# Probabilities times values in quarter-width matmuls instead of zero-padded full-width ones

## The chip, the cores and the metric

The kernel runs on one core of one Trainium2 chip, as one program. The metric is the device time of one execution in microseconds (us). The kernel before has two runs, 3971.99 and 3973.98 us, and their median, 3972.98 us, is the time to compare with.

## The reference, cut to what matters

The reference adds four blocks to x one after another: an attention, a linear layer with a low-rank update, a bidirectional state-space mixer and the linear layer again. Only the attention is touched. It has batch 8, 512 tokens, width 1024, 32 query heads of 32 and a single key and value head that all query heads share:

```
b, t, d = x.shape                                  # 8, 512, 1024
q = (x @ wq_w.T + wq_b).reshape(b, t, H, HD)       # H = 32, HD = 32
k1 = (x @ wk_w.T + wk_b).reshape(b, t, 1, HD)[:, :, 0, :]
v1 = (x @ wv_w.T + wv_b).reshape(b, t, 1, HD)[:, :, 0, :]
scores = einsum('bqhd,bkd->bhqk', q, k1) / sqrt(HD)
weights = softmax(where(causal, scores, -inf), axis=-1)
attn = einsum('bhqk,bkd->bqhd', weights, v1)       # the product that is changed
return attn.reshape(b, t, H * HD) @ wo_w.T + wo_b
```

## The kernel before, in words

The program has two parts. `attention_program` comes first and writes x1 to memory; `mixer_program` does all the rest. Each engine has its own instruction list, written out by hand, and semaphores order the engines among each other. No planner is involved.

`attention_program` first splits the weights into high and low parts (setup). Then `row(b, nxt)` handles one batch and prepares the next one: it is called once with b = None, seven times in a loop on the chip, and once for the last batch. All engines meet at a barrier between two rows.

Inside a row, the 32 heads form 8 groups (GROUPS) of 4 heads (GH), which together have 128 output features, one PSUM partition for each. The 512 query tokens form 4 tiles of 128. For query tile i, only the i + 1 key tiles up to the diagonal are computed. A *unit* is as many heads of one query tile as fit in 512 columns of scores: 4 heads for i = 0, 2 heads for i = 1, and 1 head for i = 2 and i = 3. So a group has 1 + 2 + 4 + 4 = 11 units (PER_GROUP), a row has 88, and the eight batches have 704.

The engines work on units in a pipeline. In step s of TensorE's loop (the loop over `range(UNITS + AV_LAG)`), TensorE does in this order:

- the scores of unit s: per head one matmul with q_stack as the weights and k_stack streaming (L524), and one that adds the causal mask (L526);
- in the first three units of a group, a third of the query projection of the next group (`q_part`, L464 to L466 of `split_product`);
- in one unit of a group, `finish_spread` (L484), which turns the softmax denominators of the group before;
- the transposes of the probabilities of unit s - 2 (L544);
- probabilities times values of unit s - 3 (L557), the code that is changed.

Between them, VectorE takes the maximum of each row of scores (L398), ScalarE takes the exponential (L305), and VectorE copies the transposed probabilities out of PSUM to `probs_t` (L408), which L557 waits for. `finish_scale` on VectorE (L355) reads the finished group of outputs, 128 partitions by 512 tokens in PSUM bank 6 or 7, and divides it by the denominators.

In L557 the stationary operand (the weights) is a slice of 128 columns of `v_pad`, and `probs_t` streams through in 128 columns. `v_pad` has 7 * 32 columns for each key tile: the value tile of 32 columns in the middle and zeros on both sides. A window of 128 columns that starts at `lead = (GH - 1 - j) * HEAD` puts the values at the columns of head j and zeros at those of the other three heads. Thus each matmul writes all 128 PSUM partitions of its query tile, and adds zero to those of the other heads; all heads and key tiles of a query tile form one accumulation, which starts at head 0, key tile 0. The operands are float32, and the profile shows two load-and-matmul pairs for each such product in the code. The zeros are written once at the start by GpSimd (L106), the values once per row by VectorE (L451).

Of the kernel before, what the change touches and what calls it, by code (L numbers as in the profile page):

```python
# [5 lines left out]
P = 128  # L6
# [8 lines left out]
def attention_program(nc, x, wq_t, wkv_t, wo_t, bq, bkv, kv_scale, bo, ident, ident_b, causal_b, wq_split, x1):  # L15

    BATCH, T, D = x.shape
    HEAD = wkv_t.shape[1] // 4
    TILES, CH = T // P, D // P
    GROUPS, GH = D // P, P // HEAD  # L20
# [7 lines left out]
    S_RING, P_RING, T_RING, STAT = 3, 3, 2, 8  # L28
# [12 lines left out]
    with ExitStack() as ctx:  # L41
        def sb(name, shape, dt=F32):
            return ctx.enter_context(nc.sbuf_tensor(name, shape, dt))
# [11 lines left out]
        q_hi, q_lo = sb("q_hi", [P, T], F32R), sb("q_lo", [P, T], F32R)  # L55
        q_stack = sb("q_stack", [KROWS, 2, GH, T], F32R)
        k_stack = sb("k_stack", [KROWS, T], F32R)
        v_pad = sb("v_pad", [P, TILES, 7 * HEAD])
        probs = sb("probs", [P, P_RING, T])
        probs_t = sb("probs_t", [P, T_RING, T])  # L60
        neg_max = sb("neg_max", [P, STAT, GH])
# [27 lines left out]
        with nc.Block() as block:  # L89
            @block.sync  # L90
            def _(sp):
                for n, (src, _, _) in enumerate(staged):
                    if n >= 2:
                        sp.wait_ge(staged_lo, n - 1)
                    sp.dma_start(stage(n), src).then_inc(stage_in[n % 2], DMA)
                    if 0 <= n - 3 < CH:

                        for part, w in enumerate(staged[n - 2][1:]):
                            sp.dma_start(wq_split[part, :, :, n - 3, :].rearrange("g p m -> p g m"),
                                         w.bitcast(F32).rearrange("p (g m) -> p g m", g=GROUPS)).then_inc(wq_out, DMA)  # L100
                sp.wait_ge(wq_out, 2 * CH * DMA)

            @block.gpsimd
            def _(pool):
                nc.gpsimd.memset(neg_half[:, :], -0.5).then_inc(setup_done, 1)
                nc.gpsimd.memset(v_pad[:, :, :], 0.0).then_inc(setup_done, 1)  # L106
                pool.wait_ge(params_in, 7 * DMA)
                nc.gpsimd.tensor_tensor(bkv_scaled[:, :], bkv_sb[:, :], kvs_sb[:, :], ALU.mult).then_inc(bkv_ready, 1)
                pool.wait_ge(setup_done, 2)

            @block.scalar
            def _(act):
                params = [(ident_sb[:, :], ident), (identb_sb[:, :], ident_b), (causal_sb[:, :], causal_b),
                          (bo_rows[:, :], bo), (bq_sb[:, :], bq), (bkv_sb[:, :], bkv), (kvs_sb[:, :], kv_scale)]
                for dst, src in params:
                    act.dma_start(dst, src).then_inc(params_in, DMA)
                for n, (_, hi, _) in enumerate(staged):
                    act.wait_ge(stage_in[n % 2], DMA * (n // 2 + 1))
                    nc.scalar.copy(hi, stage(n)).then_inc(staged_hi, 1)
                act.wait_ge(bkv_ready, 1)  # L120
                act.wait_ge(params_in, 7 * DMA)

            @block.vector
            def _(dve):
                for n, (_, hi, lo) in enumerate(staged):
                    dve.wait_ge(staged_hi, n + 1)
                    nc.vector.tensor_tensor(lo, stage(n), hi.bitcast(F32), ALU.subtract).then_inc(staged_lo, 1)
                dve.wait_ge(setup_done, 2)
                dve.wait_ge(params_in, 7 * DMA)

            @block.tensor
            def _(pe):
                pe.wait_ge(params_in, 7 * DMA)
                pe.wait_ge(staged_lo, len(staged))
# [22 lines left out]
        def row(b, nxt):  # L157
# [7 lines left out]
            with nc.Block(no_gpsimd_drain=True) as block:  # L165
# [168 lines left out]
                def _(dve):  # L334
# [58 lines left out]
                    if b is not None:  # L393
                        for s in range(UNITS + T_LAG):
                            if s < UNITS:
                                g, i, heads, n = unit(s)
# [45 lines left out]
                    if nxt is not None:  # L442
                        x_low(3)
                        dve.wait_ge(kv_done, 1)
                        nc.vector.tensor_copy(k_stack[:, :], att[0:KROWS, :]).then_inc(khi_done, 1)
                        dve.wait_ge(khi_done, 1)
                        low = slice(2 * HEAD, 3 * HEAD)
                        nc.vector.tensor_tensor(k_stack[low, :], att[low, :], k_stack[low, :].bitcast(F32),
                                                ALU.subtract).then_inc(k_done, 1)
                        dve.wait_ge(vt_ready, 1)  # L450
                        nc.vector.tensor_copy(v_pad[:, :, (GH - 1) * HEAD:GH * HEAD],  # L451
                                              ps[:, KV, 0:TILES * HEAD].rearrange("p (k d) -> p k d", d=HEAD)).then_inc(v_done, 1)
                        q_low(GROUPS)
                        dve.wait_ge(k_done, 1)
                        dve.wait_ge(v_done, 1)
# [5 lines left out]
                def _(pe):  # L461
# [52 lines left out]
                    if b is not None:  # L514
                        for s in range(UNITS + AV_LAG):
                            if s < UNITS:
                                g, i, heads, n = unit(s)
                                if s % PER_GROUP == 0 and g:
                                    pe.wait_ge(qs_in, g * STACK_DMAS * DMA)
                                if s >= S_RING:  # L520
                                    pe.wait_ge(exp_done, s - S_RING + 1)
                                for m, j in enumerate(heads):
                                    cols = ps[:, s % S_RING, m * n:(m + 1) * n]
                                    nc.tensor.matmul(cols, q_stack[:, g % 2, j, i * P:(i + 1) * P], k_stack[:, 0:n],  # L524
                                                     start=True, stop=False)
                                    mm = nc.tensor.matmul(cols[:, n - P:n], identb_sb[:, :], causal_sb[:, :], start=False, stop=True)  # L526
                                mm.then_inc(s_ready, 1)
                                q_unit = s % PER_GROUP
                                if q_unit < Q_UNITS and g + 1 < GROUPS:
                                    if q_unit == 0 and g:  # L530
                                        pe.wait_ge(qlo_done, g)
                                        if g >= 2:
                                            pe.wait_ge(spread_done, g - 1)
                                    q_part(g + 1, range(q_unit * CH // Q_UNITS, (q_unit + 1) * CH // Q_UNITS))
                                if (done := finishing(s, SPREAD_AT)) is not None:
                                    finish_spread(done)
                            if T_LAG <= s < UNITS + T_LAG:
                                u = s - T_LAG
                                g, i, heads, n = unit(u)
                                pe.wait_ge(exp_done, u + 1)  # L540
                                if u >= T_RING:
                                    pe.wait_ge(pt_done, u - T_RING + 1)
                                for k in range(n * len(heads) // P):
                                    mm = nc.tensor.transpose(ps[:, 4 + u % T_RING, k * P:(k + 1) * P],  # L544
                                                             probs[:, u % P_RING, k * P:(k + 1) * P], ident_sb[:, :])
                                mm.then_inc(pt_ready, 1)
                            if s >= AV_LAG:
                                u = s - AV_LAG
                                g, i, heads, n = unit(u)
                                pe.wait_ge(pt_done, u + 1)  # L550
                                if u % PER_GROUP == 0 and g >= 2:
                                    pe.wait_ge(att_done, g - 1)
                                for m, j in enumerate(heads):
                                    for k in range(i + 1):
                                        lead = (GH - 1 - j) * HEAD
                                        cols = slice(m * n + k * P, m * n + (k + 1) * P)
                                        mm = nc.tensor.matmul(ps[:, 6 + g % 2, i * P:(i + 1) * P], v_pad[:, k, lead:lead + P],  # L557
                                                              probs_t[:, u % T_RING, cols],
                                                              start=(j == 0 and k == 0), stop=(j == GH - 1 and k == i))
                                mm.then_inc(av_done, 1)  # L560
                    if nxt is not None:
                        transposes(0)
# [875 lines left out]
```

## Time and profile before

| What | Value |
|---|---|
| Runs | 3971.99 and 3973.98 us, median 3972.98 us |
| Profiled execution | span 3969.6 us; no other time of it is recorded |
| TensorE matmuls (PE) | busy 3404.7 us, 86% of the span |
| Weight loads (PEld) | busy 2841.5 us, 72% |
| VectorE (DVE), ScalarE (ACT), GpSimd (POOL) | 53%, 28%, 16% |
| L557, probabilities times values | 5120 matmuls and 5120 weight loads |
| Attention | until about 2180 us; the mixer program fills the rest |

The busy time of a matmul includes its passage through the array, so that matmuls which follow each other closely overlap in the records. The step from the start of one to the start of the next tells how fast the engine works; the duration of one record does not. In a merged line of the timeline, "x8" with a length of 1.06 us means eight instructions from the start of the first to the end of the last. A line of the timeline is: start in us, length in us, engine, line, operation, out<-in, weights (rows*columns), the streamed shape, how many, and idle time of the engine before it with what ended it.

### The profile page before, as it was taken

How to read it: one execution, taken by the hardware profiler on the slowest of the kernel's cores; microseconds unless marked ns; L12 is line 12 of the kernel's file. 1: busy time of each engine (PE TensorE's matmuls, PEld its weight loads, DVE VectorE, ACT ScalarE, POOL GpSimd, SP SyncE). 2: the span in 40 equal slices, each digit the busy share in tenths (PEclk: the TensorE clock that was granted, in tenths of full speed). 3: DMA queues.
4: the chain of work that ended last, by engine and by line, in shares of the span. 5: the costliest groups of instructions: out<-in, count | busy, mean ns of one | idle time of the engine just before them, and what ended most of it. 6: DMA issues, size and time to landing. Idle time of an engine off the chain costs nothing. (4 is left out here: it accounts for less than half of the span.)

```text
span 3969.6 us, 53353 instructions
## 1 busy us (share of the span) xinstructions
PE 3404.7 (86%) x20224; PEld 2841.5 (72%) x20224; DVE 2089.3 (53%) x3582; ACT 1116.5 (28%) x2964; POOL 618.2 (16%) x754
## 2 busy tenths in 40 slices
PE   1898998998989989989999778878787878787868
PEld 1786887887868878878788356757575757666656
DVE  3463663654636626546466236555565646464633
ACT  2341442423414414324244013121212121121221
POOL 0001001000010010000100033223232323232311
PEclk9999999999999999999999778888898988888878
DMA  6322222222222222132221400000101010101000
GB/s 213 96 75 94 79 63 96 78 70 89 75 83 75 67 93 84 60 101 79 73 75 46 154 22 22 13 31 11 33 9 34 6 38 6 37 3 41 1 21 22
DMA packets 105455, 234.99 MB, mean 59 GB/s; under 512 B 20170, under 2 KB 38858, under 8 KB 105202
## 3 DMA queue, kind: packets, MB, share of 16 engines
q1 hardware_dynamic: 100544, 228.22, 18.6%
q8 instruction: 180, 2.95, 0.3%
q10 hardware_dynamic: 4658, 3.22, 0.3%
q14 instruction: 73, 0.60, 0.0%
HBM read 139.10 MB, written 41.94 MB: 46 GB/s over the span
## 5 line engine op out<-in xcount | busy, mean ns | idle before, releaser
L305 ACT ACTIVATE probs<-ps_attn,neg_max 128x128 f32<-128x128 f32 (+3 forms) x1024 | 534.8, 526 | 1070.5 <-DVE neg_max L398 1045.5
L557 PE MATMUL ps_attn<-probs_t,v_pad 128*128 128x128 f32 x5120 | 696.3, 277 | 17.5 <-DVE probs_t L408 15.9
L557 PEld LDWEIGHTS ps_attn<-probs_t,v_pad 128*128 128x128 f32 x5120 | 626.7, 192 | 33.6 <-DVE probs_t L408 28.2
L398 DVE TENSOR_REDUCE neg_max<-ps_attn 128x1 f32<-128x384 f32 (+3 forms) x704 | 449.8, 639 | 315.9 <-PE ps_attn L526 313.7
L408 DVE COPY probs_t<-ps_attn 128x512 f32<-128x512 f32 (+1 forms) x704 | 447.1, 636 | 272.4 <-PE ps_attn L544 272.4
L1182 PE MATMUL ps_mixer<-m_w_hi,m_xt_hi 128*128 128x512 f32 x1024 | 429.0, 419 | 77.1 <-DVE m_xt_lo L1021 77.1
L524 PE MATMUL ps_attn<-k_stack,q_stack 96*128 96x128 f32 (+3 forms) x1024 | 371.1, 398 | 72.9 <-issue 50.6
L1183 PE MATMUL ps_mixer<-m_w_hi,m_xt_lo 128*128 128x512 f32 x1024 | 415.6, 406 | 0.0
L1184 PE MATMUL ps_mixer<-m_w_lo,m_xt_hi 128*128 128x512 f32 x1024 | 414.2, 405 | 0.0
L544 PE MATMUL ps_attn<-ident_sb,probs 128*128 128x128 f32 x2560 | 397.5, 274 | 0.0
L544 PEld LDWEIGHTS ps_attn<-ident_sb,probs 128*128 128x128 f32 x2560 | 285.2, 142 | 20.3
L1182 PEld LDWEIGHTS ps_mixer<-m_w_hi,m_xt_hi 128*128 128x128 f32 x1024 | 203.1, 198 | 130.6 <-DVE m_xt_lo L1021 87.7
L524 PEld LDWEIGHTS ps_attn<-k_stack,q_stack 96*128 96x128 f32 x1024 | 203.0, 201 | 78.5 <-issue 69.3
L246 POOL COPY att<-inv_den 128x512 f32<-128x512 f32 x64 | 39.3, 615 | 1395.8 <-DVE inv_den L348 1395.8
L526 PE MATMUL ps_attn<-causal_sb,identb_sb 128*128 128x128 bf16 x1024 | 233.2, 235 | 27.0 <-issue 27.0
L1021 DVE TENSOR_TENSOR m_xt_lo<-ps_mixer,m_xt_hi 128x512 fp32r<-128x512 f32 x192 | 125.7, 687 | 231.0 <-ACT m_xt_hi L933 231.0
L1184 PEld LDWEIGHTS ps_mixer<-m_w_lo,m_xt_hi 128*128 128x128 f32 x1024 | 202.6, 198 | 45.0
L1183 PEld LDWEIGHTS ps_mixer<-m_w_hi,m_xt_lo 128*128 128x128 f32 x1024 | 203.6, 199 | 42.7 <-issue 1.9
L464 PE MATMUL ps_attn<-xn_hi,wq_hi 128*128 128x512 f32 x512 | 221.0, 432 | 0.0
L466 PE MATMUL ps_attn<-xn_lo,wq_hi 128*128 128x512 f32 x512 | 205.9, 402 | 0.0
L465 PE MATMUL ps_attn<-xn_hi,wq_lo 128*128 128x512 f32 x512 | 204.1, 399 | 0.0
L933 ACT CAST m_xt_hi<-ps_mixer 128x512 fp32r<-128x512 f32 x192 | 106.1, 589 | 342.9 <-PE ps_mixer L1177 342.0
(189 smaller groups left out, 5408.3 us busy)
## 6 DMA issues: line engine op xcount, KB each, us to landing
wq_hi<-wq_split SPq DMA_DIRECT2D x64, 512.0 KB, 3.6
wq_lo<-wq_split SPq DMA_DIRECT2D x64, 512.0 KB, 4.5
q_stack<-q_hi SPq DMA_DIRECT2D x512, 64.0 KB, 2.0
x_ring<-in_a_x SPq DMA_DIRECT2D x32, 512.0 KB, 4.1
q_stack<-q_lo SPq DMA_DIRECT2D x256, 64.0 KB, 2.0
r_ring<-in_a_x SPq DMA_DIRECT2D x32, 512.0 KB, 3.7
x<-r_ring SPq DMA_DIRECT2D x32, 512.0 KB, 2.6
m_xs<-x SPq DMA_DIRECT2D x32, 512.0 KB
```

What stands on the lines that cost most here:

```text
L305: exp = nc.scalar.activation(probs[:, s % P_RING, m * n:(m + 1) * n], ps[:, s % S_RING, m * n:(m + 1) * n], ACT.Exp, bias=neg_max[:, s % S ...
L398: nc.vector.tensor_reduce(neg_max[:, s % STAT, 0:len(heads)], ps[:, s % S_RING, 0:n * len(heads)].rearrange("p (j k) -> p j k", k=n), AX.X ...
L408: nc.vector.tensor_copy(probs_t[:, u % T_RING, cols], ps[:, 4 + u % T_RING, cols]).then_inc(pt_done, 1)
L464: nc.tensor.matmul(out, a_hi, b_hi, start=first, stop=False)
L466: return nc.tensor.matmul(out, a_hi, b_lo, start=False, stop=last)
L524: nc.tensor.matmul(cols, q_stack[:, g % 2, j, i * P:(i + 1) * P], k_stack[:, 0:n], start=True, stop=False)
L526: mm = nc.tensor.matmul(cols[:, n - P:n], identb_sb[:, :], causal_sb[:, :], start=False, stop=True)
L544: mm = nc.tensor.transpose(ps[:, 4 + u % T_RING, k * P:(k + 1) * P], probs[:, u % P_RING, k * P:(k + 1) * P], ident_sb[:, :])
L557: mm = nc.tensor.matmul(ps[:, 6 + g % 2, i * P:(i + 1) * P], v_pad[:, k, lead:lead + P], probs_t[:, u % T_RING, cols], start=(j == 0 and k ...
L1182: nc.tensor.matmul(out, a_hi, b_hi, start=first, stop=False)
L1183: nc.tensor.matmul(out, a_lo, b_hi, start=False, stop=False)
L1184: return nc.tensor.matmul(out, a_hi, b_lo, start=False, stop=last)
```

## The change

`v_pad` becomes `v_sb`, which holds the 32 value columns of each key tile and nothing else. Each head's matmul takes these 32 columns as its weights and writes its own 32 PSUM partitions, `j * HEAD` to `(j + 1) * HEAD`. Each head and query tile is an accumulation of its own, over its key tiles. The two loops are exchanged: key tiles outside, heads of the unit inside. The memset of the padding is left out, and the count that is waited for in the setup goes from 2 to 1. Everything else, the number of matmuls among it, stays.

```
-        v_pad = sb("v_pad", [P, TILES, 7 * HEAD])
+        v_sb = sb("v_sb", [P, TILES, HEAD])
...
-                nc.gpsimd.memset(v_pad[:, :, :], 0.0).then_inc(setup_done, 1)
...
-                pool.wait_ge(setup_done, 2)
+                pool.wait_ge(setup_done, 1)
...
-                dve.wait_ge(setup_done, 2)
+                dve.wait_ge(setup_done, 1)
...
-                        nc.vector.tensor_copy(v_pad[:, :, (GH - 1) * HEAD:GH * HEAD],
+                        nc.vector.tensor_copy(v_sb[:, :, :],
                                               ps[:, KV, 0:TILES * HEAD].rearrange("p (k d) -> p k d", d=HEAD)).then_inc(v_done, 1)
...
-                                for m, j in enumerate(heads):
-                                    for k in range(i + 1):
-                                        lead = (GH - 1 - j) * HEAD
+                                for k in range(i + 1):
+                                    for m, j in enumerate(heads):
                                         cols = slice(m * n + k * P, m * n + (k + 1) * P)
-                                        mm = nc.tensor.matmul(ps[:, 6 + g % 2, i * P:(i + 1) * P], v_pad[:, k, lead:lead + P],
-                                                              probs_t[:, u % T_RING, cols],
-                                                              start=(j == 0 and k == 0), stop=(j == GH - 1 and k == i))
+                                        mm = nc.tensor.matmul(ps[j * HEAD:(j + 1) * HEAD, 6 + g % 2, i * P:(i + 1) * P],
+                                                              v_sb[:, k, :], probs_t[:, u % T_RING, cols],
+                                                              start=(k == 0), stop=(k == i))
                                 mm.then_inc(av_done, 1)
```

## Rows read from the trace of the kernel before

**Rows 1.** Page: busy time and share of the span of each engine.

```profile
PE 3404.7 (86%) x20224; PEld 2841.5 (72%) x20224; DVE 2089.3 (53%) x3582; ACT 1116.5 (28%) x2964; POOL 618.2 (16%) x754
```

**Rows 2.** Windows, one batch and the mixer: PE, PEld, DVE, ACT, POOL; clock; DMA.

```profile
392.00:658.00 266.00, 248.09 (x1714) 216.99 (x1712) 141.64 (x242) 91.73 (x286) 17.57 (x20) 0.97 0.26 80
...
2300.00:3970.00 1670.00, 1358.12 (x6360) 1076.14 (x6360) 899.27 (x1585) 344.65 (x621) 472.44 (x580) 0.86 0.07 20
```

**Rows 3.** Page, groups: shapes, count, busy us, mean ns, idle before.

```profile
L557 PE MATMUL ps_attn<-probs_t,v_pad 128*128 128x128 f32 x5120 | 696.3, 277 | 17.5 <-DVE probs_t L408 15.9
L557 PEld LDWEIGHTS ps_attn<-probs_t,v_pad 128*128 128x128 f32 x5120 | 626.7, 192 | 33.6 <-DVE probs_t L408 28.2
```

**Rows 4.** Timeline of TensorE over one unit of query tile 3.

```profile
708.96 0.28 PE L557 MATMUL ps_attn<-probs_t,v_pad 128*128 128x128 f32 x1
708.99 0.42 PE L524 MATMUL ps_attn<-k_stack,q_stack 96*128 96x384 f32 x1
709.25 0.23 PE L526 MATMUL ps_attn<-causal_sb,identb_sb 128*128 128x128 bf16 x1
709.32 0.61 PE L544 MATMUL ps_attn<-ident_sb,probs 128*128 128x128 f32 x4
709.77 1.06 PE L557 MATMUL ps_attn<-probs_t,v_pad 128*128 128x128 f32 x8
710.58 0.42 PE L524 MATMUL ps_attn<-k_stack,q_stack 96*128 96x384 f32 x1
```

**Rows 5.** Timeline around L585: transposes of 32 rows between full-width matmuls.

```profile
613.64 0.39 PE L465 MATMUL ps_attn<-xn_hi,wq_lo 128*128 128x512 f32 x1
...
613.86 0.39 PE L466 MATMUL ps_attn<-xn_lo,wq_hi 128*128 128x512 f32 x1
614.18 0.32 PEld L585 LDWEIGHTS ps_attn<-ident_sb,att 32*128 32x128 f32 x4 [0.35 <-issue]
614.18 0.43 PE L585 MATMUL ps_attn<-ident_sb,att 32*128 32x32 f32 x4
...
614.54 0.50 PE L464 MATMUL ps_attn<-wo_hi,at_hi 128*128 128x512 f32 x1
...
614.88 0.39 PE L465 MATMUL ps_attn<-wo_hi,at_lo 128*128 128x512 f32 x1
```

**Rows 6.** Timeline around L1228: 48 weight columns between matmuls of 128.

```profile
2455.35 0.19 PEld L1227 LDWEIGHTS ps_mixer<-m_h_next,m_p_wx_t 128*128 128x128 f32 x1 [0.24 <-issue]
...
2455.78 0.19 PEld L1227 LDWEIGHTS ps_mixer<-m_h_next,m_p_wx_t 128*128 128x128 f32 x1 [0.24 <-issue]
...
2456.73 0.17 PEld L1228 LDWEIGHTS ps_mixer<-m_h_next,m_p_wbc_t 128*48 128x48 f32 x2 [0.76 <-issue]
2456.73 1.06 PE L1228 MATMUL ps_mixer<-m_h_next,m_p_wbc_t 128*48 128x512 f32 x2
...
2457.72 1.06 PE L1230 MATMUL ps_mixer<-m_p_wdt_t,m_h_next 128*128 128x8 f32 x8
...
2458.61 0.19 PEld L1182 LDWEIGHTS ps_mixer<-m_xt_hi,m_wd_hi 128*128 128x128 f32 x1
```

**Rows 7.** Timeline around L1262: weights of 16 rows between full ones.

```profile
2423.03 1.04 PE L1253 MATMUL ps_mixer<-m_c_ident,m_x_feat 128*128 128x128 f32 x8
...
2424.00 1.15 PE L1262 MATMUL ps_mixer<-m_c_feat,m_b_feat 16*128 16x128 f32 x8
...
2425.08 1.95 PE L1267 MATMUL ps_mixer<-m_p_fcd_t,m_x_feat 128*128 128x4 f32 x16
...
2426.89 0.47 PE L1272 MATMUL ps_mixer<-m_dt_reach,m_c_later 128*128 128x128 f32 x2
```

**Rows 8.** Instructions of L795: loads of 40 weight columns, ns min/median/max.

```profile
L795 PEld LDWEIGHTS ps_mixer<-m_xs,m_wsum x32: 112/117/186, 2228.3 to 2250.4; 128*40 128x40 f32 x32
```

**Rows 9.** Instructions that write v_pad: copy per row, memset; ns, start us.

```profile
L451 DVE COPY v_pad<-ps_attn x8: 291/292/293, 106.4 to 1953.0; 128x128 f32<-128x128 f32 x8
L106 POOL MEMSET v_pad<- x1: 844/844/844, 0.8 to 0.8; 128x896 f32 x1
```

## The prediction

> **What bounds the kernel now.** I read the busy shares first: TensorE's matmuls are busy 86% of the span, VectorE 53%, and no other engine is above that but TensorE's own weight loads [rows 1]. The windows then say where. One batch of the attention takes 266 us, and TensorE is busy 248.09 us of it; VectorE has 141.64 us. The granted clock is 0.97 there, so TensorE is nearly always at the higher of its two levels, 2.4 GHz; in the mixer it is 0.86 [rows 2]. Third, the group list: in all 5120 matmuls of L557, TensorE sat idle for only 17.5 us, 15.9 of them waiting for probs_t [rows 3]. The attention's loop is bound by how fast TensorE gets through its own list. A microsecond taken from or added to TensorE there moves the end by a microsecond; VectorE and ScalarE have slack.
>
> How fast L557 goes is read from starts, not from durations. In one unit eight instructions span 1.06 us, and one record lasts 0.275; the other seven steps take 0.785 us, 0.112 us each. The next unit's scores follow 0.81 us after the first, without a gap [rows 4]. All of L557 is thus 5120 x 0.112 = 573 us of TensorE's time, and not the 696.3 us of its busy column.
>
> Is that step set by the load or by the streaming? By both. A 512-column float32 matmul takes 0.43 us from one to the next (the loads at 2455.35 and 2455.78) [rows 6], so 128 columns stream in 0.107. Full-width loads of L1230, which has only 8 columns to stream, are eight in 0.97 us of 0.19 each: 0.11 us a step [rows 6]. A load of 40 columns lasts 117 ns in the median against 192 for 128 columns [rows 3, 8], 0.85 ns less for each of the 88 columns; a load of 32 columns, 96 fewer, therefore costs about 0.03 us instead of 0.11 (an estimate). **The first thing to see is that this gains nothing by itself:** the load was hidden behind a stream of equal length, and the stream keeps its 128 columns and its count. At most 0.112 - 0.107 = 0.005 us a step are left, 5120 x 0.005 = 26 us; I take none of it, since no row tells whether the load or the stream makes it.
>
> **The part that costs.** The change puts narrow matmuls between full-width ones, and the trace has three places of that kind.
> - L1228 has 48 weight columns. Loads normally run one matmul ahead. The second matmul of L1227 starts at 2456.21 and streams until 2456.64; the narrow load starts only at 2456.73, 0.09 late, and nobody is waited for. Then a load of 48 columns lies bare (0.04), two streams take 0.86, and the load of the full-width L1230 starts 0.09 after that (2457.72), bare again for 0.11. In and out: 0.09 + 0.04 + 0.09 + 0.11 = 0.33 us [rows 6].
> - L585, four transposes of 32 rows. A full 512-column step before it is 613.64 to 613.86, 0.22. From 613.86 to 614.88 there are two such steps and four transposes of about 0.07: 0.73 of 1.02 us, so 0.29 are lost [rows 5].
> - L1262, weights of 16 rows: from 2423.03 to 2426.89 there are 32 instructions of 0.11, 3.52 of 3.86 us, 0.34 lost; with the 0.107 of the streams of 4 columns it is 0.37 [rows 7].
>
> In each, TensorE empties before it takes a matmul of the other size, and the load that would have been hidden is bare. With a bare load of 32 columns on the way in (0.03) the three give 0.32, 0.26 and 0.26 to 0.29. I take 0.30, near the first, which like the change has few columns and float32; the ends are 0.26 and 0.37. A step of TensorE's loop goes from scores and transposes (full width) into L557 and back, once a unit. There are 704 units; in each of the 8 batches the last unit's values follow the second last's with nothing between, which takes away 8: 696 visits. 696 x 0.30 = **+209 us**, with nothing beside it to hide it, because TensorE is the bound.
>
> **The part that gains.** In units with several heads, neighbouring matmuls now have their own weight columns and their own PSUM partitions. The trace has no such pair, so it must be bounded. From below: nothing overlaps, and each takes its 0.112 as today: 0. From above: a head's stream runs beside another's, while the two instructions of one head follow each other. A unit of query tile 0 (4 heads, 8 instructions) then goes A1, A2+B1, B2+C1, C2+D1, D2: 5 steps instead of 8. A unit of query tile 1 (heads A, B, A, B) is 5 instead of 8 as well. That is 3 steps x 0.112 = 0.34 us in 3 of the 11 units of a group, 64 x 3 x 0.336 = **-64 us**. The other 8 units of a group have one head, whose matmuls all go to the same 32 partitions: nothing to gain, and these hold 28 of the 40 products. I take the upper end: emptying the engine for 48 columns [rows 6] makes sense only if the array is then split into parts that work by themselves. The exchange of the loops alone costs nothing: the same instructions in another order between the same waits.
>
> The Trainium skill says so too: "TensorE: Matmul & The Clock Gate", Part 3, tells of three column tiles of 32 that ran 2.38 times as fast together; no run here shows it yet. By the page's rule the sum has the 64 us, without it none.
>
> **The small parts.** Part of the 15.9 us in which L557 waited for probs_t [rows 3] will now lie beside the emptying: -10 us, between 0 and -16. The memset of 0.84 us ran at 0.8 us from the start, long before the first copy into the same tile at 106.4 us, and the copy of the values (0.29 us, once a batch) keeps its 128 elements a partition [rows 9]: 0, and were they not hidden, under 3 us. VectorE's L355 still waits for the last unit of a group.
>
> **The sum.** 209 - 64 - 10 = +135 us on the profiled span of 3969.6 us. The median of the runs is 3.4 us above that span, so the time is 3969.6 + 135 + 3.4 = **4108 us**, 3.4% slower. With the ends (181 - 64 - 16 and 257 - 64 - 5) this case runs from 4074 to 4161.
>
> **The rivals.** A measurement of this kernel tells about 2% (79 us) from no change; the bounds are 3893 and 4052.
> - *Nothing overlaps.* The heads of a unit queue up as before. For it: no row has two matmuls at once. Against it: the reason above. 209 - 10: 4172 us, 4141 to 4230.
> - *No emptying, and so not slower.* The 0.09 us gaps come from the change of rows in L585 and L1262, and in L1228 from the odd width of 48, and a quarter of 32 columns is taken without a stop. Then -64, and perhaps the 20 us that a short load leaves of 0.112 to 0.108: 3889 to 3909 us. Below about 0.10 us a visit it ends under the time of before (0.10 x 696 = 70). Against it: three shapes show the gap, and the one without a change of rows has the same. If only one of the two directions costs (0.20 for the way back), 139 - 64 - 10: 4038 us, within 2%.
> - *Each move to another quarter empties too.* There are 3 such moves in a unit of query tile 0 and 3 in each of the two of tile 1, 9 x 64 = 576 at 0.12: +69 on the case without overlap, 4241 us. No row shows moves of this kind. The Trainium skill, "TensorEngine Tiling (Array Packing)", Key Properties, says that only changing the mode drains the engine, not changing the tile; by it this rival falls.
> - *The narrow loads don't run ahead, or the clock falls.* Were the 0.03 us of a load bare in each of 5120, +143 on the case without overlap: 4315. Against it: the two loads of L1228 together take 0.17 us, so the second ran ahead of its matmul [rows 6]. Were the attention's granted clock 0.86, as in the mixer, instead of 0.97 [rows 2], its 2050 us would be 13% longer: +262, 4370 us.
>
> **How the numbers follow.** Chances: forecast 0.48; nothing overlaps 0.24; no emptying or half of it 0.17, of which 0.05 end faster by over 2%; each move empties 0.04; loads or clock 0.07. Slower by over 2%: 0.48 + 0.24 + 0.04 + 0.07 = 0.83; within 2%: 0.12; faster: 0.05. The range goes from the forecast's low end down to the half-price case at 4038 and up past 4241: 4030 to 4250, which leaves out the 0.07 above and some 0.12 below. The forecast case alone is 4074 to 4161.
>
> **What would show it.** In the changed profile, in a unit of query tile 3, the eight matmuls of L557 should still be 0.11 us apart; the load of the first should start about 0.09 us after the transposes' last stream, and the next L524's load 0.09 after the last stream of L557, unit length 1.6 to 1.9 us. Loads of L557 should last about 105 ns. In a unit of query tile 0 pairs of matmuls should start closer than 0.107; if they are 0.11 apart, the second case holds. A batch should take 266 + 17 = 283 us, with the mixer unchanged. I am wrong if L557's load is pulled ahead into the transposes, or if the granted clock in the attention leaves 0.97.

## The result, and the profile after

The changed kernel takes 4048.3 us (median of 4040.08 and 4056.52), against 3972.98 us before: 1.0198 times as long, 95% interval 1.0171 to 1.0226. That is +75 us. The forecast was +135 us (4108 us), with a range of 4030 to 4250 us. The direction holds, and so does the cost of each visit, where a *visit* is one change of TensorE from full-width matmuls to narrow ones and back. Two sizes were off: the gain from overlap was put too small, and the first and last groups of a batch were counted like the middle ones. The measured time lies under the forecast case's own span of 4074 to 4161 us; only the wider range holds it.

The profiled execution has a span of 4038.3 us, 68.7 us more than before. The first view is the page: shares of the engines and the group of the changed line, which is now L555.

```profile
PE 3485.5 (86%) x20224; PEld 2688.3 (67%) x20224; DVE 2091.6 (52%) x3582; ACT 1114.5 (28%) x2964; POOL 617.1 (15%) x753
...
L555 PE MATMUL ps_attn<-probs_t,v_sb 128*32 128x128 f32 x5120 | 593.7, 277 | 12.4 <-DVE probs_t L407 11.1
...
L555 PEld LDWEIGHTS ps_attn<-probs_t,v_sb 128*32 128x32 f32 x5120 | 406.3, 109 | 131.8 <-issue 109.5
...
L523 PEld LDWEIGHTS ps_attn<-k_stack,q_stack 96*128 96x128 f32 x1024 | 199.2, 197 | 205.4 <-issue 200.9
```

The same loads of the scores in the kernel before, where the line is L524:

```profile
L524 PEld LDWEIGHTS ps_attn<-k_stack,q_stack 96*128 96x128 f32 x1024 | 203.0, 201 | 78.5 <-issue 69.3 <-DMA q_stack<-q_lo 8.1
```

Against [rows 1, 3]: the loads of 32 columns last 109 ns instead of 192, and the matmuls' busy time fell from 696.3 to 593.7 us. A reader who stops there expects a faster kernel. The cost stands in the last column of the weight loads: 109.5 us "issue" before L555 and 200.9 us before L523, the full-width load that follows it. Before the change L557's loads had no such entry, and L524's had 69.3 us. "Issue" here is TensorE running empty: nothing is waited for, but the load doesn't run ahead.

The windows place the loss. One stretch of a batch, and the mixer:

```profile
395.00:671.00 276.00, 259.77 (x1725) 198.81 (x1724) 142.38 (x243) 92.45 (x289) 16.41 (x21) 0.98 0.25 77
...
2300.00:4038.00 1738.00, 1396.44 (x6432) 1088.70 (x6432) 927.89 (x1621) 355.46 (x634) 474.94 (x584) 0.86 0.09 27
```

A batch takes 276 us instead of 266, and the granted clock (0.98 and 0.86) is within 0.01 of before [rows 2]. From the records, the attention's last matmul ends at 2292.3 us instead of 2215.1: +77.2 us. What comes after it took 1746.0 instead of 1754.4 us; that part also varied between 1738 and 1764 us over the twelve kernels profiled here, none of which touches it. Its 8.4 us less are why the span rose by 68.7 us and not by 77.2.

Now one unit with one head, in the timeline (a unit of query tile 3, to compare with [rows 4]):

```profile
723.85 0.60 PE L543 MATMUL ps_attn<-ident_sb,probs 128*128 128x128 f32 x4
724.37 0.79 PEld L555 LDWEIGHTS ps_attn<-probs_t,v_sb 128*32 128x32 f32 x8 [0.17 <-issue]
724.37 1.06 PE L555 MATMUL ps_attn<-probs_t,v_sb 128*32 128x128 f32 x8
...
725.36 0.19 PEld L523 LDWEIGHTS ps_attn<-k_stack,q_stack 96*128 96x128 f32 x1 [0.20 <-issue]
```

A length of one matmul record is 0.27 us, of which 0.11 is its streaming. The last transpose starts at 723.85 + 0.60 - 0.27 = 724.18 and streams 0.11 us, until 724.29; the narrow load starts at 724.37, 0.08 later. The eight matmuls span 1.06 us as before, 0.11 us a step: with one head nothing got faster. The first of them can stream only behind its load, at about 724.40, so the eighth ends at about 725.28; the wide load comes at 725.36, again 0.08 later, and then lies bare (no streaming hides it). The ends of the streams are worked out here, not recorded.

And the units with several heads:

```profile
704.91 0.43 PE L555 MATMUL ps_attn<-probs_t,v_sb 128*32 128x128 f32 x8
705.27 0.44 PE L523 MATMUL ps_attn<-k_stack,q_stack 96*128 96x384 f32 x1
...
706.15 0.63 PE L555 MATMUL ps_attn<-probs_t,v_sb 128*32 128x128 f32 x8
706.71 0.44 PE L523 MATMUL ps_attn<-k_stack,q_stack 96*128 96x384 f32 x1
```

Eight matmuls in 0.43 us (four heads) and in 0.63 us (two heads), instead of 1.06. The single records start at 704.912, .919, .926 and .932, then at 705.046, .052, .059 and .066: four streams at once, two steps in all. With two heads it is four steps.

The best measure is the length of each of TensorE's steps, from the first scores of one unit to those of the next, worked out from the start times (medians over groups 1 to 6 of the eight batches, the first being group 0; us). Step r does the scores of unit r and the values of unit r - 3, so that step 3 has the four heads, steps 4 and 5 the pairs:

```
step      0      1      2      3      4      5      6      7      8      9      10     sum
before    3.472  3.913  3.902  1.587  1.587  1.478  2.195  1.312  1.312  1.423  1.772  23.95
after     3.758  4.206  4.196  1.245  1.448  1.342  2.487  1.605  1.609  1.712  1.932  25.54
change   +0.29  +0.29  +0.29  -0.34  -0.14  -0.14  +0.29  +0.29  +0.30  +0.29  +0.16   +1.59
```

The price of a visit is 0.293 us, the median of the seven steps with the values of one head and no wait (0.286 to 0.297). With it taken off, four heads gain 0.635 us and each pair 0.43. In step 10 L557 had waited 0.13 us for probs_t before the change; that wait now lies beside the emptying.

### The profile page after: what moved, and what is told of

Its sections match the earlier page's. It is cut to its first block and busy times, and to the rows that moved or that the text cites. A ratio compares the mean times of both kernels' runs of the same rounds, so it can differ in the third digit from the quotient of the medians.

```text
span 4038.3 us, 53352 instructions
## 1 busy us (share of the span) xinstructions
PE 3485.5 (86%) x20224; PEld 2688.3 (67%) x20224; DVE 2091.6 (52%) x3582; ACT 1114.5 (28%) x2964; POOL 617.1 (15%) x753
## 5 line engine op out<-in xcount | busy, mean ns | idle before, releaser
L555 PE MATMUL ps_attn<-probs_t,v_sb 128*32 128x128 f32 x5120 | 593.7, 277 | 12.4 <-DVE probs_t L407 11.1
L555 PEld LDWEIGHTS ps_attn<-probs_t,v_sb 128*32 128x32 f32 x5120 | 406.3, 109 | 131.8 <-issue 109.5
L523 PE MATMUL ps_attn<-k_stack,q_stack 96*128 96x128 f32 (+3 forms) x1024 | 383.5, 411 | 67.5 <-issue 50.4
L523 PEld LDWEIGHTS ps_attn<-k_stack,q_stack 96*128 96x128 f32 x1024 | 199.2, 197 | 205.4 <-issue 200.9
L463 PE MATMUL ps_attn<-wo_hi,at_hi 128*128 128x512 f32 x512 | 201.4, 393 | 0.0
```

The lines of the kernel that those rows point to most:

```text
L463: nc.tensor.matmul(out, a_hi, b_hi, start=first, stop=False)
L555: mm = nc.tensor.matmul(ps[j * HEAD:(j + 1) * HEAD, 6 + g % 2, i * P:(i + 1) * P], v_sb[:, k, :], probs_t[:, u % T_RING, cols], start=(k = ...
```

## The experiments

The first four take the two terms apart. Their times stand against runs of the kernel before on the same chip (median 3968.45 us).

**e1_hybrid**: narrow only where it gains.

```
+ if len(heads) > 1:
+     ... matmul(ps[j * HEAD:(j + 1) * HEAD, ...], v_pad[:, k, (GH - 1) * HEAD:GH * HEAD], ..., start=(k == 0), stop=(k == i))
+ else:
+     ... the padded full-width matmul of before
```

> Narrow matmuls only in the three units of a group that hold several heads (query tiles 0 and 1); the eight units with one head keep the padded full-width weights. Theory 'price per visit, full overlap' (a change between full and narrow matmuls costs 0.29 us in and out; heads with partitions of their own run fully side by side, 2 steps instead of 8 with four heads, 4 instead of 8 with two): the steps with query tile 0 and 1 keep what the changed kernel showed, -0.34, -0.14 and -0.14 us, all others return to the time of before. That is -0.62 us in each of 64 groups, -30 to -40 us on 3973: 3933 to 3943 us. Rival 'the gain came from elsewhere' (for instance from the narrow single-head units): then this kernel is slower than before, +0.29 x 3 x 64 = +56 us, 4029.

Measured: 3953.18 us, ratio 0.9968 (0.9950 to 0.9986), -13 us: the right side, less than half the size. The steps: -0.36, -0.14 and -0.14 us in steps 3 to 5, within about 0.02 of before in all the others but one. Step 10 was 1.772 us in every group; now it lies between 1.77 and 2.97 us, 2.26 in the mean, and takes back 0.49 of the 0.64 us gained. A group of the middle takes 23.83 us in the mean instead of 23.95. The timeline at the end of a group shows why:

```profile
452.26 1.16 PE L564 MATMUL ps_attn<-probs_t,v_pad 128*128 128x128 f32 x8
454.24 0.33 PE L524 MATMUL ps_attn<-k_stack,q_stack 96*128 96x128 f32 x1 [0.82 <-DMA q_stack<-q_lo]
```

The next group's scores wait for the copies of the queries into q_stack. The twelve copies are issued by SyncE one after another; in the same group:

```profile
443.53 4.95 SPq L188 DMA_DIRECT2D q_stack<-q_hi  x8
448.53 2.50 SPq L188 DMA_DIRECT2D q_stack<-q_lo  x4
```

A second chain, from the projection through q_hi and these copies to the scores, is about as long as TensorE's own 23.95 us a group was. Most of the gain went into waiting for it; e9_hybrid_q2 below tests this.

**e2_outer**: the changed kernel with heads outside, key tiles inside.

```
-for k in range(i + 1):
-    for m, j in enumerate(heads):
+for m, j in enumerate(heads):
+    for k in range(i + 1):
```

> The changed kernel with the loops the other way round: heads outside, key tiles inside, so that in a unit of two heads all four instructions of one head come before those of the other. Only the units of query tile 1 differ, 2 of 11. Theory 'each quarter has a queue of its own, deep enough': the second head starts at once, nothing changes, within 5 us of the changed kernel. Rival 'the streams start in program order': the second head starts only with the last instruction of the first, 7 steps instead of 4, 3 x 0.112 x 2 x 64 = +43 us on the changed kernel, about 4090 us; the steps with query tile 1 grow from 1.34 and 1.45 us to 1.68 and 1.78.

Measured: 4042.63 us, ratio 1.0199 (1.0167 to 1.0231), the same ratio as the changed kernel; steps 4 and 5 are 1.453 and 1.347 us. A unit of two heads:

```profile
708.80 0.64 PE L555 MATMUL ps_attn<-probs_t,v_sb 128*32 128x128 f32 x8
```

Its records start at 708.801, .815, .935 and .948. In the program the second head comes behind four instructions of the first, and yet something starts 14 ns after the first instruction. It can't be the first head's own second one, since those are 0.11 us apart wherever a head is alone. The records don't name the head, but eight matmuls in 0.64 us are four steps, as before the exchange. So each quarter works off its own instructions, and the start in program order, on which the forecast's count of steps rested, does not hold. The exchange of the two loops is worth nothing either way.

**e3_half**: 64 weight columns, heads 0 and 1 in the lower and 2 and 3 in the upper 64 partitions.

```
+lead, low = (1 - j % 2) * HEAD, j // 2 * 2 * HEAD
+matmul(ps[low:low + 2 * HEAD, ...], v_pad[:, k, lead:lead + 2 * HEAD], ..., start=(j % 2 == 0 and k == 0), stop=(j % 2 == 1 and k == i))
```

> Half-width instead of quarter-width: weights of 64 columns, 32 of them zero padding, and each head writes 64 partitions (heads 0 and 1 the lower, 2 and 3 the upper half). The two heads of a unit of query tile 1 then share their partitions. Theory 'price per visit, overlap only between different partitions': 0.29 + 0.03 (a bare load of 64 instead of 32 columns) in every visit; query tile 1 gains nothing (+0.32 us a step against before), query tile 0 has 4 to 7 steps instead of 8. Sum per group 11 x 0.32 - 0.45 at most = 3.1, less some 0.13 that lies beside the wait for q_stack: +2.9 us a group, +150 to +190 us, 4125 to 4160 us. Rival 'only quarters make the engine empty': no price here, 3973 or less.

Measured: 4120.12 us, ratio 1.0376 (1.0348 to 1.0405), 5 us under the expected range and far from the rival's 3973. Steps with one head grew by 0.32 or 0.33 us, 0.03 more than with 32 columns, which is what a longer bare load would add (argued, not tested alone). The two steps with pairs, whose heads now share their partitions, grew by 0.32 as well: no overlap within the same partitions. Step 3 changed by -0.10: a gain of 0.42, nearly 4 of 8 steps, since two halves run side by side. The price isn't one of quarters; it is that of leaving the full width.

**e4_twice**: in units of query tile 3 four matmuls ahead of the transposes, four behind.

```
+if s >= AV_LAG and unit(s - AV_LAG)[1] == TILES - 1 and T_LAG <= s < UNITS + T_LAG:
+    values(s - AV_LAG, 0, 2)
...
+values(u, 2 if twice else 0, i + 1).then_inc(av_done, 1)
```

> The changed kernel, but in each unit of query tile 3 (4 of 11) the eight matmuls are cut in two: four ahead of the transposes of the step, four behind them. Same instructions, one visit more in these steps. Theory 'price per visit': +0.29 us in each of these steps, 4 x 0.29 = 1.17 us a group, about +70 us on the changed kernel, 4120 us. Rival 'the price is paid per narrow instruction' (3.2 us of a group's 80 instructions, 0.04 each): the count is the same, 0, 4048 us.

Measured: 4115.36 us, ratio 1.0367 (1.0339 to 1.0395), 67 us above the changed kernel's median. Steps 10, 0, 1 and 2, which do these units, grew by 0.26, 0.28, 0.24 and 0.27 us over the changed kernel; the others by nothing. With the instructions the same, the price belongs to the visit. The same cut with full-width weights was not run; that cutting alone costs nothing is argued from the kernel before, which goes from transposes into L557 and on without a gap [rows 4].

The next runs look for what the change would be worth with few visits, and for the second chain (kernel before on that chip: 3972.99 us, for the last two 3975.45 us).

**e6_before_q2**: the kernel before, `Q_UNITS = 2` instead of 3.

> The kernel before with one number changed: the query projection of the next group is done in the first two units of a group instead of the first three (Q_UNITS 2). The control for the next kernel. Theory 'the copies into q_stack are a second chain, nearly as long as TensorE's own work' (12 copies of 0.63 us each to issue, 11.4 us from the end of the projection to the first scores of the next group): the projection ends some 1.5 us earlier, so the remaining wait of about 0.35 us a group for q_stack goes: -15 to -20 us, 3950 to 3958. Rival 'the copies don't matter': 3968.

Measured: 3962.3 us, ratio 0.9969 (0.9952 to 0.9987), -11 us: less than the theory's 15 to 20. A group went from 23.95 to 23.86 us only. The 0.35 us of waiting for the copies that I had put into step 10 is not there: step 10 is 1.772 us before and 1.773 here, longer than step 9 by 0.22 for 8 matmuls of values instead of 6 and by the 0.13 of waiting for probs_t. The copies hardly bound the kernel before, except at the start of a batch, where the first groups together got 3.6 us shorter.

**e9_hybrid_q2**: the hybrid with `Q_UNITS = 2`.

> The hybrid (narrow only where a unit has several heads) with the projection in two units as well. The hybrid gained 0.64 us a group in its units, and its last step of a group grew by 0.69. Theory 'that step waits for the copies into q_stack': with the chain 1.5 us shorter the gain comes out, 0.62 + 0.35 us a group against the kernel before, about 51 groups' worth: -50 us, 3918; against its control -32 us. Rival 'the step grew for another reason, for instance a wait for the values or the clock': no more than the control gains, 3945 to 3955.

Measured: 3938.59 us, ratio 0.9915 (0.9895 to 0.9935). Step 10 is back at 1.773 us and the group at 23.26 us, 0.60 under its control e6_before_q2. In these groups the whole gain of the three units comes out once the second chain is shorter: that chain had hidden it in e1_hybrid. The time is 24 us under the control and not the 32 expected, and far from the 3918: seven of the eight last groups of a batch gain nothing (25.6 us from their first scores to their last values in both). Against the kernel before it is -0.69 us a group, not the 0.97 expected, by the 0.35 that was never there.

**e5_grouped**: three visits a group instead of 11, all narrow. probs_t gets four slots, the two PSUM banks of the transposes stay. TOGETHER says after which unit a visit comes and how many units it serves; the lines left out skip the units of other query tiles.

```
+T_BANKS = 2
+TOGETHER = {2: 3, 6: 4, 10: 4}
...
+if s >= AV_LAG and (s - AV_LAG) % PER_GROUP in TOGETHER:
+    units = range(u - TOGETHER[u % PER_GROUP] + 1, u + 1)
+    for i in sorted({unit(v)[1] for v in units}):
+        for k in range(i + 1):
+            for v in units:
+                ...
+                for m, j in enumerate(heads):
+                    ... matmul(ps[j * HEAD:(j + 1) * HEAD, ...], v_sb[:, k, :], probs_t[:, v % T_RING, cols], start=(k == 0), stop=(k == i))
```

> Narrow matmuls with three visits a group instead of 11: the values of the three units of query tiles 0 and 1 are done together, then those of the four units of tile 2, then the four of tile 3, heads side by side (probs_t has 4 slots instead of 2). Theory 'price per visit, full overlap': 3 x 0.29 = 0.9 us, and 2 + 4 + 6 + 8 = 20 steps of 0.111 instead of 80: TensorE's work falls from 23.6 to 17.7 us a group. Then the chain through the projection and the copies into q_stack ends last: 8.2 + 11.4 = 19.6 us a group. 3968 - 4.3 x 51 = 3750 us (TensorE alone would allow 3660). Rival 'VectorE or the waits between engines bind first' (VectorE has 16.4 us of work a group): above 3800. Rival 'overlap needs heads of one unit': no gain from it, 80 steps less the present ones: about 3900.

Measured: 3941.12 us, ratio 0.9928 (0.9906 to 0.9950). Faster, but by 32 us instead of 220; of the three numbers on record the rival's 'above 3800' for waits between the engines holds. The matmuls did what was expected of them: in two visits,

```profile
487.64 1.08 PE L562 MATMUL ps_attn<-probs_t,v_sb 128*32 128x128 f32 x32
491.78 0.86 PE L562 MATMUL ps_attn<-probs_t,v_sb 128*32 128x128 f32 x24 [0.40 <-DVE probs_t L409]
```

32 matmuls in the time of 8. The time went into waits, and into the clock. TensorE's waits, and a stretch of three batches with its granted clock:

```profile
PE ps_attn L525 <- DMA q_stack<-q_lo: 108.9, 56, 3.1
...
PE ps_attn L545 <- ACT probs L306: 71.7, 152, 2.0
...
PE ps_attn L562 <- DVE probs_t L409: 41.7, 72, 1.8
```

```profile
1000.00:1800.00 800.00, 671.19 (x5298) 530.98 (x5298) 422.11 (x744) 279.71 (x890) 53.35 (x61) 0.93 0.26 81
```

TensorE waited 108.9 us for q_stack against 6.6 before, and between 132 and 2000 us the clock was at its lower level, half of the higher, for 280 us in 52 pieces, against 96 us in 7 before. The 184 us more at half the clock are worth up to 92 us (an estimate). A group takes 23.2 us in the mean instead of the 19.6 that I had for the chain; the estimate took TensorE's share of it at the full clock and left out the waits for ScalarE and VectorE. How the difference divides between these was not tested.

**e8_grouped_q2**: grouped, `Q_UNITS = 2`.

> The grouped kernel with the projection in two units. If the chain through q_stack ends last, each group gets 1 to 1.5 us shorter: 18.2 to 18.6 us, 3680 to 3700 us. If VectorE or something else binds, no change against the grouped kernel.

Measured: 3825.53 us, ratio 0.9633 (0.9613 to 0.9653). The chain was what ended last in e5_grouped: a group falls to 20.7 us in the mean (20.4 in the median) and the wait for q_stack from 108.9 to 15.7 us. The same edit was worth 11 us in e6_before_q2 and is worth 116 here. With the waits went part of the lower clock, 167 us instead of 280, so up to some 56 of the 116 us came back that way (an estimate as above). It is still above the 3680 to 3700 expected. What is late next:

```profile
PE ps_attn L545 <- ACT probs L306: 86.4, 166, 2.0
...
PE ps_attn L562 <- DVE probs_t L409: 76.1, 72, 1.8
...
1000.00:1800.00 800.00, 674.47 (x5542) 537.18 (x5543) 453.93 (x799) 296.14 (x925) 57.14 (x70) 0.95 0.27 82
```

TensorE now waits for the exponentials and the copies, yet neither engine is full: VectorE is busy 57% and ScalarE 37% of these 800 us. What is late seems to be a unit's way round through maximum, exponential, transposes and copy, not an engine's rate; this is read from the shares and was not tested.

**e7_pairs_q2**: as e8_grouped_q2 with `TOGETHER = {0: 1, 2: 2, 4: 2, 6: 2, 8: 2, 10: 2}`, six visits.

> As the grouped kernel with the projection in two units, but six visits a group instead of three: unit 0 alone, then pairs of units. The heads of a pair lie side by side, so the streams are 2 + 4 + 12 + 16 = 34 steps of 0.111 instead of 20, and the visits cost 6 x 0.29. TensorE's own work is 23.6 - 8.9 + 3.8 + 1.7 = 20.2 us a group, against 17.7 with three visits, but no long stretch keeps the scores from the other engines. Theory 'price and overlap, and the grouped kernel waits 2.7 us a group for VectorE and ScalarE': about 20.3 to 20.6 us a group, level with the grouped kernel's 20.4, 3815 to 3845 us. Rival 'the waits come with any grouping': 22 us a group or more, above 3880.

Measured: 3871.13 us, ratio 0.9744 (0.9713 to 0.9776): between the two theories in time, and at 22.0 us a group on the rival's side. The wait for probs_t was 94.8 us in 160 pieces: each visit also waits for the copy of its last unit, and six visits wait more often than three. That waits come with any grouping is the better half of the answer.

**e10_grouped_q1**: grouped, `Q_UNITS = 1`.

> The grouped kernel with the whole projection of the next group in its first unit (Q_UNITS 1). In the version with two units the wait for q_stack had fallen from 108.9 to 15.7 us and the waits for ScalarE and VectorE (86 and 76 us) were what was left. Theory 'VectorE and ScalarE bind now': within 15 us of that version, or slower since TensorE holds back the scores for 5.5 us at once: 3820 to 3850. Rival 'the chain through q_stack still binds': another 1 us a group less, 3770 to 3790 us.

Measured: 3811.5 us, ratio 0.9599 (0.9567 to 0.9631), 4% faster than the kernel before, the best of all. It is 14 us under the version with two units, between the two theories and nearer to the first, whose range began at 3820. The two stand against different runs of the kernel before. A group of the middle is the same within 0.1 us (20.60 us in the mean against 20.68); of the 14 us, 10 lie in the first groups of the batches (193.4 us for the eight instead of 203.2). No wait for q_stack of over 0.15 us is left, the wait for probs_t fell from 76.1 to 52.0 us, and the wait for the exponentials rose from 86.4 to 120.8 us:

```profile
PE ps_attn L545 <- ACT probs L306: 120.8, 168, 2.0
```

So the chain through q_stack is no longer the bound, and the waits for the other engines are. How many of them a longer ring of probs_t, or a longer lag between a unit's scores and its transposes, would remove was not tried.

## Why the prediction was right, and where its sizes were off

- **TensorE bounds the attention, so its lost time shows in full.** Right for the 48 middle groups: each takes 23.95 us before and 25.54 after, +1.59 x 48 = 76 us. Wrong for the 16 others. The eight first groups, with waits for q_stack at the start of a batch, take 212.5 us together before and 210.6 after, -2; they scatter by more than the change (26.38 and 26.86 in one batch, 28.46 and 26.92 in the next). In a last group the steps up to its last scores grow by 0.66 us, from 18.68 to 19.34, but from its first scores to its last values it takes 25.6 and then 25.9 us: the rest lies beside waits, and the eight add 2 us. What lies ahead of, between and behind these groups adds 1. That makes the 77. The forecast counted both ends of a batch like the middle.
- **A microsecond taken from TensorE moves the end by a microsecond.** Wrong: in e1_hybrid 0.64 us a group were taken and 0.12 came out, since the chain through q_stack was about as long.
- **The short load gains nothing.** Right within 2 ns: with one head most steps are 0.111 or 0.112 us before and 0.109 or 0.110 after.
- **The price of a visit.** Forecast 0.30 us, measured 0.293; 696 x 0.293 = 204 us, against the 209 of the sum. e4_twice shows that it is paid per visit, e3_half that it comes with 64 columns too. The rivals without emptying and with half of it fall.
- **The overlap.** This term was mis-sized: -64 us was forecast, from 3 of 8 steps hidden in each of the three units. The steps give (0.635 + 2 x 0.43) x 64 = -96 us. The step that failed is the order A1, A2+B1, B2+C1 and so on, which let a head start only when the one ahead of it had started its last instruction. e2_outer shows that the quarters don't wait for each other: four heads take 2 steps, two take 4. The rival "nothing overlaps" falls, and so does "each move to another quarter empties": the moves are 7 ns apart. The Trainium skill's span for such a pack ("TensorE: Matmul & The Clock Gate", Part 3: the duration of one matmul and about 4 ns for each tile more) fits the mechanism, with 7 ns here. Its 2.38 times for three tiles is further from full overlap than e5_grouped, where 32 matmuls over four quarters took the time of 8.
- **The wait for probs_t.** -10 us was forecast, beside the emptying. It was there, 0.13 us in step 10 of each group, 8 us.
- **Together:** 204 - 96 - 8 = +100 us if every group were like the middle ones, against the +135 of the sum; 32 of the 35 us between are the overlap. The ends of the batches take it to the +77 of the attention's records.
- **Luck in the range.** 4048.3 us is below the 4074 at which the forecast case ended. The range holds it because it was drawn down to the rival in which only one direction costs (4038 us), and that rival's mechanism is not what happened: the price was paid nearly in full. The direction was earned; that the range held the time was partly luck.
- **Small slips in the sums.** With the 16 us of the low end, 'nothing overlaps' starts at 4138 and not 4141 us, and its +143 for bare loads takes 0.028 us for each of 5120, not 0.03. Neither touches the forecast.
- **The clock** stayed where it was (0.98 against 0.97), and narrow loads ran ahead of their matmuls, so these two rivals fall.

What stays open: how much of the 0.29 us is the emptying and how much the bare loads is read from starts (0.08 and 0.08, the rest loads), not tested alone. That TensorE runs empty is itself read from these gaps.

## What to carry to other kernels

A matmul of few columns between full-width ones has a fixed price, here 0.29 us in and out, so collect narrow work until one visit holds enough of it, and from as many different partition quarters as there are: 4 heads in one visit repay it, one head never does. Before counting on such a gain, look for the chain that is nearly as long as the bound; here waiting for the copies into q_stack took about four fifths of the first 0.6 us a group, and moving the projection earlier gave it back. When a matmul's zero padding is removed, ask whether the number of columns that stream changes; if not, the zeros cost next to nothing, here 2 ns a step.

## What the runs showed of the hardware

- Matmuls into different quarters start 7 ns apart (with two heads in e2_outer 14 ns) and don't keep to the program's order among the quarters (e2_outer); 32 of them took 1.08 us, as 8 in one quarter do.
- Weights of 32 columns run ahead of the matmuls in flight though all use the same 128 rows: eight loads in 0.79 us beside eight matmuls. One line of the Trainium skill ("TensorE: Matmul & The Clock Gate", Part 3) says that loads overlap with running matmuls only when the row group differs; the text above it there also allows a background weight buffer. The trace agrees with the second and not with the first.
- In e5_grouped the clock fell to its lower level 52 times between 132 and 2000 us, most of them after TensorE had stood still for 1.3 to 2.9 us, against 7 times before, once between every two batches. A faster TensorE that then waits can pay part of its gain back through the clock.
